# A second buffer for X3, and the last batch's cproj, sum and third layer norm ahead of mlp2 and output of the batch before

## The reference

```python
shift_a, scale_a, gate_a, shift_m, scale_m, gate_m = split(silu(c) @ W_mod + b_mod, 6)
q, k, v = split(modulate(ln(x), shift_a, scale_a) @ W_qkv + b_qkv, 3)
x = x + gate_a * (softmax(q k^T * scale) v @ W_proj + b_proj)
q_c = ln(x) @ W_qc + b_qc;  k_c, v_c = split(ln(context) @ W_kvc + b_kvc, 2)
x = x + softmax(q_c k_c^T * scale) v_c @ W_cproj + b_cproj
h = gelu(modulate(ln(x), shift_m, scale_m) @ W_mlp1 + b_mlp1) @ W_mlp2 + b_mlp2
x = x + gate_m * h
```

## Time and profile before

| | |
|---|---|
| median of 3 runs | 1509.5 us (1508.64 to 1513.65) |
| the profiled execution | 1505.56 us |
| its span, first to last instruction | 1503.3 us |
| mean granted TensorE clock | 0.972 |
| TensorE busy | 1380.9 us (92%) |
| VectorE, ScalarE, GpSimd busy | 1111.4 (74%), 1094.2 (73%), 705.6 (47%) |

### The profile page before, as it was taken

The page is one execution under the profiler, slowest core; times in us unless marked ns, Lnnn a source line. Parts: engine busy times, 40 slices in busy tenths (PEclk is TensorE's granted clock), DMA queues, the critical chain, the costliest instruction groups (busy, mean ns, idle before and its releaser), DMA issues.

```text
span 1503.3 us, 39974 instructions
## 1 busy us (share of the span) xinstructions
PE 1380.9 (92%) x15090; PEld 910.1 (61%) x15090; DVE 1111.4 (74%) x1992; ACT 1094.2 (73%) x1852; POOL 705.6 (47%) x995
## 2 busy tenths in 40 slices
PE   2577899999999999999999999999999999999775
PEld 1234466666666666666666666666666666665544
DVE  4647887788777777788777788778777777775543
ACT  3244687777777888778778888778778888777551
POOL 2233344455545554455554554455554554445421
PEclk8779999999999999999999999999999999999988
DMA  5122233333323333333323323333333232322110
GB/s 178 50 72 87 88 94 96 97 106 101 99 91 99 89 97 98 96 105 105 99 91 100 91 91 101 97 100 109 96 95 97 90 96 95 99 91 67 52 50 15
DMA packets 142133, 137.97 MB, mean 92 GB/s; under 512 B 38070, under 2 KB 116567, under 8 KB 141943
## 3 DMA queue, kind: packets, MB, share of 16 engines
q1 hardware_dynamic: 141942, 135.42, 29.0%
HBM read 56.34 MB, written 9.55 MB: 44 GB/s over the span
## 4 chain that ended last, share of the span: by engine, by line
PE 77%; DVE 9%; DMA 4%; ACT 3%; issue 3%; POOL 2%; SPq 2%; DVEq 0%; ACTq 0%; POOLq 0%
PE dense_ps L348 15%; PE dense_ps L350 13%; PE dense_ps L349 13%; PE o_ps L696 13%; PE max_ps L661 10%; PE exp_ps L678 7%; PE dense_ps L596 4%; DVE mx_cross L1015 3%; DVE mx_self L1015 2%; DMA o_rb_cross<-r_dram_cross 2%; ACT probs L818 1%; SPq L433 1%; DMA r_dram_cross<-o_r_cross 1%; PE dense_ps L623 1%; POOL Y L1179 1%
## 5 line engine op out<-in xcount | busy, mean ns | idle before, releaser
L818 ACT ACTIVATE probs<-exp_ps 128x1024 f32<-128x1024 f32 x512 | 525.3, 1026 | 189.0 <-PE exp_ps L678 186.5
L1015 DVE TENSOR_REDUCE mx_cross<-max_ps 128x4 f32<-128x1024 f32 x256 | 313.4, 1224 | 101.8 <-PE max_ps L661 94.2
L1015 DVE TENSOR_REDUCE mx_self<-max_ps 128x4 f32<-128x1024 f32 x256 | 312.3, 1220 | 78.5 <-PE max_ps L661 76.4
L1150 POOL TENSOR_TENSOR o_n_self<-o_n_self,o_rb_self 128x512 f32<-128x512 f32 x32 | 40.5, 1266 | 292.9 <-DMA o_rb_self<-r_dram_self 292.9
L1183 POOL TENSOR_TENSOR g_split<-G,g_split 128x512 f16<-128x512 f32 x120 | 136.5, 1159 | 58.5 <-ACT g_split L807 58.5
L348 PE MATMUL dense_ps<-mlp_hi,g_split 128*128 128x256 f16 x504 | 140.2, 278 | 5.1 <-DVE g_split L1093 5.1
L348 PE MATMUL dense_ps<-xt,mlp_hi 128*128 128x256 f16 x512 | 140.8, 275 | 3.0 <-DVE xt L979 2.8
L349 PE MATMUL dense_ps<-xt,mlp_hi 128*128 128x256 f16 x512 | 140.5, 274 | 0.0
L350 PE MATMUL dense_ps<-xt,mlp_lo 128*128 128x256 f16 x512 | 140.4, 274 | 0.0
L350 PE MATMUL dense_ps<-mlp_hi,g_split 128*128 128x256 f16 x504 | 139.6, 277 | 0.0
L349 PE MATMUL dense_ps<-mlp_lo,g_split 128*128 128x256 f16 x504 | 139.5, 277 | 0.0
(11 more groups left out here) (230 smaller groups left out, 3337.3 us busy)
## 6 DMA issues: line engine op xcount, KB each, us to landing
q_stack_self<-split_q SPq DMA_DIRECT2D x192, 64.0 KB, 2.6
k_stack_self<-split_k SPq DMA_DIRECT2D x192, 64.0 KB, 2.6
k_stack_cross<-split_kc SPq DMA_DIRECT2D x192, 64.0 KB, 2.6
q_stack_cross<-split_qc SPq DMA_DIRECT2D x192, 64.0 KB, 2.6
X<-in_x SPq DMA_DIRECT2D x32, 256.0 KB, 2.8
Ctx<-in_ctx SPq DMA_DIRECT2D x32, 256.0 KB, 3.2
rows_a<-rows_a_dram SPq DMA_DIRECT2D x32, 256.0 KB, 3.4
o_n_self<-o_sb_self SPq DMA_DIRECT2D x64, 128.0 KB, 2.8
```

The lines of the kernel that those rows point to most:

```text
L818: nc.scalar.activation(probs[:, t % 8:t % 8 + 2], exp_ps[:], ACT.Exp).then_inc(exp_taken[kind], 2)
L1015: nc.vector.tensor_reduce(mx[kind][:, :, :, t // 2].rearrange("p q a -> p a q"), max_ps[:].rearrange("p a (q k) -> p a q k", q=2), AX_X, A ...
L1150: nc.gpsimd.tensor_tensor(o_n[kind][:], o_n[kind][:], o_rb[kind][:], ALU.mult).then_inc(o_mult[kind], 1)
```

## The change

X3 gets two buffers, chosen by `b.u`, and every reader and writer of it names its own. `x3` of batch n now waits for `y_add` of batch n - 2. In the table of the last batch four steps are moved: cproj from slot 1131 to 1119, just ahead of mlp2_0 of batch 30 (TensorE); x3 and ln3 from 1137 to 1121, behind the last split and ahead of y of batch 30 (VectorE); norm3 from 1140 to 1122, ahead of y_add of batch 30 (GpSimd). t3 of batch 31 and all behind it keep their slots. In banks the order of tenants stays the same.

```diff
     31: {"max_cross": 2, "exp_cross": 8, "k": -1, "k_hi": -1, "r_back_self": 1, "qc_lo": 1, "normc": 4,
         "split_cross": 2, "m_cross": 3, "m_copy_cross": 4, "o_gather_cross": 7, "o_recip_cross": 8,
-        "o_norm_cross": 2, "o_hi_cross": 2, "cproj": -4, "x3": -10, "ln3": -9, "norm3": -8, "t3": -8, "t3_hi": -8,
+        "o_norm_cross": 2, "o_hi_cross": 2, "cproj": 8, "x3": 6, "ln3": 7, "norm3": 10, "t3": -8, "t3_hi": -8,
...
-        X3 = sb("X3", [P, 2, D])
+        X3 = sb("X3", [P, 2, 2, D])
...
-                    wait_count(dve, y_done, b.n)
-                    nc.vector.tensor_tensor(X3[:].rearrange("p t d -> p (t d)"), bank("cproj"),
+                    wait_count(dve, y_done, b.n - 1)
+                    nc.vector.tensor_tensor(X3[:, b.u].rearrange("p t d -> p (t d)"), bank("cproj"),
                                             XC[:, b.u].rearrange("p t d -> p (t d)"), ALU.add).then_inc(taken["cproj"], 1)
...
-                    statistics(b, "3", X3)
+                    statistics(b, "3", X3[:, b.u])
...
-                        nc.vector.tensor_tensor(Y[:, t], Y[:, t], X3[:, t], ALU.add).then_inc(y_done, 1)
+                        nc.vector.tensor_tensor(Y[:, t], Y[:, t], X3[:, b.u, t], ALU.add).then_inc(y_done, 1)
...
-                    nc.gpsimd.tensor_tensor(X3[:], X3[:], rows_b[:, b.u, 1:2].to_broadcast([P, 2, D]), ALU.add
+                    nc.gpsimd.tensor_tensor(X3[:, b.u], X3[:, b.u], rows_b[:, b.u, 1:2].to_broadcast([P, 2, D]), ALU.add
...
-                    normalise(b, "3", X3)
+                    normalise(b, "3", X3[:, b.u])
...
-                    nc.gpsimd.tensor_tensor(Y[:], Y[:], X3[:], ALU.add).then_inc(y_done, 1)
+                    nc.gpsimd.tensor_tensor(Y[:], Y[:], X3[:, b.u], ALU.add).then_inc(y_done, 1)
```

## The result

The changed kernel took 1498.76 us (median of 7 runs, 1494.44 to 1502.73), the kernel before 1509.52 us in the same measurement (1508.64 to 1513.65). The ratio is 0.992, with a 95% interval of 0.9901 to 0.9939: faster by 9 to 15 us, where 7.8 were forecast. Two later measurements of the same kernel gave 0.9932 (0.9915 to 0.9949) and 0.9935 (0.9919 to 0.9952), some 10 us.

The account below looks back on a forecast made before the run. TensorE, busy 92% of the span, was taken as the bound, with gains only in the last three slices. 6.62 + 0.45 + 0.3 + 0.4 = 7.8 us gave 1501.7 us; 8-in-10 range 1497.5 to 1505.5.

Parts of the forecast that it names:

- the first term: Last batch on TensorE: t3 of batch 31 starts at 1476.92 instead of 1483.54, a gain of 6.62 us.
- The four signs of the new order: Tail profile: cproj near 1467.5, X3's sum right behind the splits, norm done 1.5 us before t3, t3 without idle time.
- The sign for the clock: TensorE in mlp1 of batch 31: starts near 1479.5, low clock for about 16 matmuls after 1480.5.
- one sign of being wrong: The forecast is wrong if the middle before 1460 moves by more than 1 us.
- The second term: From t3 to mlp1 of batch 31: 2.59 us at full clock instead of 3.04, a gain of 0.45 us.
- The third term: Clock in mlp1 and mlp2: falls as before, 1.7 us lost in mlp1 instead of 2.0, a gain of 0.3 us.
- rival A: Clock doesn't fall at 1470.2, before mlp2 of batch 30: 1500.2 us, or 1498.5 if mlp1 escapes too; chance 0.18.
- the likeliest case: The forecast itself for the whole kernel: 1501.7 us, own range 1499.5 to 1504.5; chance 0.67.
- The fourth term: Second buffer in the other batches: x3 of batch 29 starts 0.48 us earlier, a gain of 0.4 us.
- B: Clock falls before t3 and stays low through all 48 matmuls of mlp1: gain 4.0 us, 1505.5; chance 0.08.
- D: Earlier x3 of batch 29 shifts work behind 1412 into low-clock stretches of 1.7 us each: slower, 1514; chance 0.03.
- C: Something else holds x3 or norm3 of batch 31 until mlp2 of batch 30 is done: 1.5 us gained, 1508; chance 0.04.

Follow-up runs that it names:

- the two filled kernels: The kernel before and the changed kernel, each with unread matmuls added in TensorE's idle stretches of the tail: ratios 0.9987 and 0.9932.
- buffer and cproj: Changed kernel with only the two X3 buffers and the early cproj of batch 31; x3, ln3 and norm3 at their old places: ratio 0.9979.
- norm3 late: Changed kernel, but norm3 of batch 31 stays behind y_add of batch 30 on GpSimd: ratio 0.9981.
- stand-in: Kernel before plus 12 unread matmuls ahead of mlp2 of batch 30, waiting for ot_cross as cproj would; cproj stays late: ratio 0.999.
- changed second: The changed kernel run again without edits, for a second profile: ratio 0.9932, tail 25.27 us.
- both further kernels: Changed kernel with t3 of batch 31 ahead of mlp2's last part of batch 30; one also moves the sum ahead of two splits: 0.9926 and 0.9937.
- changed third: The changed kernel run once more without edits, for a third profile: ratio 0.9935, tail 27.78 us.
- before again: The kernel before run again without edits, for a second profile of its tail: ratio 1.0006, tail 37.40 us.
- buffer alone: Kernel before with only the two X3 buffers added, the last batch's steps at their old places: ratio 1.0004.
- the kernel reordered further: Changed kernel with t3 of batch 31 ahead of mlp2's last part of batch 30, and the sum ahead of the last two splits: ratio 0.9937.
- The kernel with t3 ahead of part 3: Changed kernel with t3 of batch 31 ahead of mlp2's last part of batch 30, sum still behind the fourth low split: ratio 0.9926.

## Why the prediction was right or wrong

**The mechanism and the first term** were right. The four signs of the new order came: cproj 0.05 us behind ot_cross, X3 behind the splits without a wait, the normalised rows 0.7 us before t3 (1.5 had been foreseen, against an mlp2 with more low matmuls), and t3 without idle time. The 6.62 us measured 6.56, between the two filled kernels (14.47 - 7.91). The sign for the clock did not come: there was no low clock in mlp1, where some 16 low matmuls were foreseen. And one sign of being wrong did appear, a middle that moved by more than 1 us: t3 of batch 29 stood 2.8 us later, at 1420.13 where it was at 1417.31. The unchanged kernel run again had it at 1422.07, 4.8 us later, so that sign was narrower than the scatter between executions and says nothing on the change.

**The second term**, 0.45 us from t3 to mlp1 by the higher clock, measured 0.45 to 0.52 (3.04 and 3.05 to 2.53 and 2.59). Right.

**The third term was mis-sized; this is the step that failed**: "again I let it fall, with some 16 matmuls low", 0.3 us. In mlp1 of batch 31 the clock fell in none of the three profiles of the changed kernel, while 19 and 24 matmuls had run low in the two before; from mlp1's start to the end this is 1.9 and 2.4 us, at or past the upper bound of 2.0 that the forecast had given. The fall was put at the time at which it came in the old order, 2.1 us into an idle stretch of 5.14; in the new order the 48 matmuls of mlp2 run right up to the transposes, and the idle stretch behind these is over after 1.93 us. For mlp2 of batch 30 the forecast took "keeps its 6.9 us" from one profile. From the anchor to the end of mlp2 (to y) the two kernels took 9.71 and 10.73 before, and 8.74, 8.05 and 10.66 changed: a mean gain of 1.1 us, with executions in which there is none. Together the clock, second term included, is worth 4.0 and 5.5 us in the tail of the old order and 0.6, 0.0 and 2.5 in the new, so 3.8 us on the mean where the second and third terms had 0.75. With 6.56 this makes 10.3, the difference of the mean tails (36.6 - 26.3). That the parts add up tests nothing, since the clock's part is each tail less that of the filled kernel.

So what happened lies at **rival A** with its extension to mlp1 (1498.5), which had been given 0.18 as a whole, and not at the likeliest case. That 1498.76 fell so close to it is in part luck: mlp1 escaped the low clock in all three profiles, but mlp2 of batch 30, A's own event, escaped it wholly in one of three. The reading that failed is that of one row: the fall 2.1 us behind cproj's matmuls in the profile before was taken as what such a pair of work and idle time does. It does so at times, and the two cases are not alike: in the old order dense mlp2 matmuls ran straight into cproj and all the idle time came behind, in the new one 1.92 to 2.42 us of it lie ahead of cproj and 0.34 to 1.06 behind. Ahead of mlp2 of batch 30, with 12 matmuls in the middle of the idle stretch, the clock stayed up in six profiles (buffer and cproj, norm3 late, stand-in, changed second, both further kernels) and was low for a part in two (changed, and changed third). Without them it was low in all three (before, before again, buffer alone).

The rule of the Trainium skill ("TensorE: Matmul & The Clock Gate", Part 1), that the clock drops after a wholly idle monitoring window, spoke for rival A and was the better guide to the usual case. The traces do not bear it out to the letter: in two of the eight profiles the clock fell though cproj's matmuls lay in the stretch. What the rows add is the idle time just ahead of the 12 matmuls. It was 2.42 and 2.33 us in the two profiles in which the clock fell, and 1.68 to 2.10 in the six in which it didn't; it depends on how long after mlp1 of batch 30 the ot_cross of batch 31 is ready. The row of the changed kernel's third profile, beside the one of the first above:

```profile
1470.17 0.28 PE L348 MATMUL dense_ps<-cproj_hi,ot_cross 128*128 128x256 f16 x1 [2.33 <-DVE ot_cross L1029]
```

No run varied this stretch on purpose, so that it decides is not shown and stays open.

**The fourth term**, the earlier x3 of batch 29, has its local size. From the first matmul of cproj of batch 29 to its t3, the profiles with one buffer took 6.60, 6.61 and 6.61 us (the one of the stand-in 6.25, since x3 came late enough there not to wait), those with two 6.11 to 6.25. In the changed kernel x3 waits 0.19 us, for TensorE:

```profile
1415.54 0.69 DVE L1043 TENSOR_TENSOR X<-dense_ps,XC 128x512 f32<-128x512 f32 x1 [0.19 <-PE dense_ps L350]
```

Whether its 0.4 us reach the end can't be shown: from that t3 to the anchor the profiles scatter from 49.2 to 51.0 us with one buffer and from 49.5 to 51.3 with two, and the buffer alone gave 1.0004.

**The rivals B to D** did not come about. C in particular is out by the rows of X3 above, and B by mlp1's window. D's price has a slip: eight stretches of 1.7 us are 13.6 us, 5.8 more than the gain and not 4.5; nothing else rests on it.

## What to carry to other kernels

When an order of work is changed at a kernel's thin end, cost the hole twice: once for the wait, by the rows, and once for the clock, by what the hole does to the matmuls behind it; here, by the tails, the second was more than half of the first (3.8 and 6.56 us). A clock's place in one profile is one throw: take a second profile of the same kernel, or fill the holes with matmuls whose result nobody reads, in both orders, before a term rests on it. And in a chain that crosses four in-order queues move every link; one left behind cost most of the gain.

## What the runs showed of the hardware

- Low and high matmuls in the same place in different executions of the same kernel: 14, 0 and 27 low ones between anchor and t3 in three profiles of the changed kernel, 16 and 26 of the kernel before. The changed kernel's tail moves with them by up to 2.5 us (25.27 to 27.78).
- An idle stretch of 1.93 us between four transposes and mlp1, behind 48 dense matmuls of mlp2, left the clock at 1.00 in all three profiles of the changed kernel. Idle stretches of 4.2 to 5.1 us, ahead of mlp2 of batch 30 or of t3 of batch 31, had a low clock behind them each time: nine stretches, in six profiles.
- In the kernel reordered further, GpSimd's two smallest instructions took 0.53 and 0.52 us, where they take 0.19 in the same place in every other profile. They ran while VectorE wrote the low splits, an instruction with two operands in SBUF (the two splits end at 1476.48 and 1477.08, the two small instructions 0.05 us behind them):

```profile
1475.82 1.26 DVE L1098 TENSOR_TENSOR g_split<-G,g_split 128x512 f16<-128x512 f32 x2
```
```profile
1476.00 0.53 POOL L1138 TENSOR_SCALAR ve<-mv 128x2 f32<-128x2 f32 x1 [13.73 <-DVE mv L969]
1476.62 0.52 POOL L1139 TENSOR_SCALAR nm<-mv 128x2 f32<-128x2 f32 x1
```

The kernel with t3 ahead of part 3 differs from this one only in that these two splits stand ahead of the sum, so nothing runs beside the small instructions. There they take:

```profile
1479.44 0.19 POOL L1138 TENSOR_SCALAR ve<-mv 128x2 f32<-128x2 f32 x1 [14.34 <-DVE mv L969]
1479.72 0.19 POOL L1139 TENSOR_SCALAR nm<-mv 128x2 f32<-128x2 f32 x1
```

This is the 0.7 us by which that kernel's norm was late. The Trainium skill ("GPSIMD Engine Reference", section 1, Specifications) says that the two engines share their SBUF interfaces and contend when VectorE reads two SBUF inputs; the rows agree. The pair of kernels shows that running beside the splits is what costs the 0.7 us; that the shared interfaces are the reason is what the Trainium skill says, and no run here tests it.
